# A four-layer cross-attention chain: wide attention scores for one head of two tiles per unit, the rarer expert as a weight difference, VectorE's softmax in half of all units

## The chip, the cores and the metric

The kernel runs on 1 core of one Trainium2 chip. The metric is the device time of that core in microseconds (us), from start to end of one execution. Engines are called PE (TensorE), DVE (VectorE), ACT (ScalarE), POOL (GpSimd) and SP (SyncE, which issues the transfers here).

## The reference

There are 64 batch entries of 64 tokens with 256 channels (x), and as many context tokens with 128 channels (ctx). Four layers follow each other.

```python
# L0: one-head attention of x over ctx @ W_mem, a sigmoid gate, RMS norm
# L1: LayerNorm, then 16 heads of 64 channels over ctx (masked), tanh-gated residual; LayerNorm, GELU MLP of 1024
# L2, L3, each:
vm  = expert_mask(types)                  # token and its successor are both of type 1
x   = rms_norm(h)
mixed = where(vm, x @ v_qkv, x @ l_qkv)   # 16 heads of 16 channels, rotary, causal attention
h   = h + where(vm, ctx @ v_dense, ctx @ l_dense)
h   = h + cross_attention(rms_norm(h))    # 16 heads of 8 channels over the context
mi  = rms_norm(h)
v_out = silu(mi @ v_gate) * (mi @ v_up) @ v_down
l_out = silu(mi @ l_gate) * (mi @ l_up) @ l_down     # 688 hidden channels
h   = h + where(vm, v_out, l_out)
```

In the inputs only tokens 48 to 63 of an entry can be of expert v; all others are of expert l. Everything is computed in f32.

## The kernel before

**Tiles and streams.** The 64 entries are eight groups of 8 entries (512 tokens; activations lie with channels on partitions, so a tile is 128x512). Two groups are in flight as streams a and b; four turns of both streams make the whole. Stream b runs about half a layer behind a, so that the attention of one stream lies beside the MLP of the other. In one turn the phases are, in this order: wide attention (L1) of a beside L0 of b; L1's MLP and L2 attention of a beside L1 of b; L2 attention of b beside the L2 MLP of a; L3 attention of a beside the L2 MLP of b; L3 attention of b beside the L3 MLP of a; L3 MLP of b beside L0 of the next a.

**Order.** `schedule` runs in Python when the program is made. It takes steps with nominal times (`l1_stage`, `attention_stage`, `ffn_stage` and so on), a cost table for each engine (`parts`) and dependencies (`follows`), and writes one fixed order of steps for each engine. Each engine then works its list strictly in that order and waits on semaphores. Where the planner expects PE to wait, it puts in filler products (`pause`, L966), whose results nobody reads.

**Wide attention, L1.** It has eight tiles j of two heads each (`l1_stage`). In each, `l1k` computes K (PE L1200, then two half-height ACT copies into a block-diagonal buffer, L1487, which `zero_k` on POOL has cleared, L1843), `l1v` computes V (L1211), `l1q` computes Q (L1220). `scores` makes one unit of 128x512: first the media mask as a bf16 product with 2 rows (L1013), then 8 products of 128 rows, 64 columns of weights and 128 streamed columns (L1017), which compute both heads at once thanks to the zeros in K. `prob` and `trans` (four transposes, L1057), `pv` (16 products in two 64x64 quarters, L1074) and `wo` (L1227) follow.

**Softmax.** There are two ways. ACT's way: DVE takes the maximum (L1639), ACT makes eight exponentials of 64 columns each with a sum (L1438). DVE's way (`by_vector`): DVE takes the maximum, subtracts it (L1644), ACT makes one exponential of 512 columns (L1431), DVE sums (L1653). Then DVE's reciprocal (L1655) and POOL's product (L1839) end both. Even units of L2 and L3 attention go DVE's way, and all of L1 goes ACT's. Four units fit into the buffer `Ebuf`. Units of L2 and L3 are made in pairs on two PSUM banks: the causal mask as two bf16 products of 64 rows (L1024), then 8 products of 64 rows, 64 weight columns and 256 streamed columns, which take the four 64x64 quarters in turn (L1033).

**Experts.** The activations are kept twice, masked: `xn` times `is_l` and `xv` times `is_v`. After a norm, DVE multiplies by the gains (`spread`, L1716), then by `is_l` (L1726 or L1729), then the late tokens by `is_v` (L1733), and POOL the others (L1853). PE adds l weights times `xn` and v weights times `xv`; for v only the 16 late tokens of each entry are streamed (L986, L1340, L1361). In the MLP, for each of 6 hidden chunks (`g`, `silu`, `u`, `down`): ACT copies g and takes a tanh, DVE makes the SiLU (L1796), multiplies by u (L1809), by `is_l` (L1814), the late tokens by `is_v` (L1815), and POOL the early tokens by `is_v` (L1881). `down` waits for these. MLP weights come from HBM through a ring of five slots (`load_chunk`, on SP), six transfers a chunk.

Of the kernel before, what the change touches and what calls it, by code (L numbers as in the profile page):

```python
# [14 lines left out]
P = 128  # L15
B, S, D, E = 64, 64, 256, 128
G = 8
# [47 lines left out]
def l0_stage():  # L65
    steps = [(0, "load"), (0, "masks"), (0, "x", 0), (0.5, "x", 1), (1.0, "ctx"), (3.0, "mem", 0), (3.9, "mem", 1),
             (4.8, "memN", 0), (5.7, "memN", 1), (7.0, "scores", ("l0", 0)), (9.5, "prob", ("l0", 0)),
             (12.0, "trans", ("l0", 0)), (14.0, "l0pv", 0), (15.0, "l0pv", 1), (16.0, "zero_k"), (17.0, "gate", 0),
# [4 lines left out]
def l1_stage():  # L73
    steps = []
    for j in range(JT):
        at = 8.7 * j
        steps += [(at, "l1k", j), (at + 0.9, "l1v", j), (at + 1.8, "l1q", j), (at + 3.9, "scores", ("l1", j)),
                  (at + 6.0, "prob", ("l1", j)), (at + 12.1, "trans", ("l1", j)), (at + 13.7, "pv", ("l1", j)),
                  (at + 24.5, "wo", j)]
# [3 lines left out]
    for j in range(JT):  # L83
        for k, (when, step) in enumerate(((0.5, ("trans", ("l1", j))), (2.0, ("pv", ("l1", j))), (5.0, ("wo", j)))):
            if step not in done:
                steps.append((end + when + 0.1 * j, *step))
# [50 lines left out]
def ffn_stage(n):  # L137
    steps = []
    for j in range(FT):
        steps += [(6.4 * j, "g", n, j), (6.4 * j + 1.5, "silu", n, j), (6.4 * j + 2.1, "u", n, j), (6.4 * j + 10.6, "down", n, j)]  # L140
    return steps + [(6.4 * FT + 6.4, "res3", n)], 6.4 * FT + 6.4
# [58 lines left out]
FILLER, HOP, SLACK, LEAD, REACH = 0.3, 0.2, 0.1, 10.0, 80.0  # L200
BULK = ("g", "silu", "u", "down", "l1h", "w2")
# [3 lines left out]
def parts(step, where):  # L205
# [6 lines left out]
    if step == "scores":  # L212
# [3 lines left out]
        if kind != "l1":  # L216
            return chain(("PE", 0.02 if where[0][2] % 2 else {"self": 1.35, "cross": 1.05}[kind]), *softmax)
        return chain(("PE", 1.35), *softmax)
# [12 lines left out]
    if step == "spread":  # L231
        own = chain(("PE", 0.3 if n in HALVED else 0.45), ("DVE", {0: 1.5, 1: 2.45, 2: 2.45, 4: 0.95, 7: 0.95, 5: 2.0, 8: 2.0}.get(n, 3.45)))
# [5 lines left out]
    if step == "keys":  # L238
        return [("POOL", 2.15, None)]
    if step == "u":  # L240
        return chain(*(() if where[1] == FT - 1 else (("PE", 2.2),)), ("DVE", 2.4), ("POOL", 1.4))
    if step == "g" and where[1] == FT - 1:
# [4 lines left out]
        "zero_k": (("POOL", 1.8),), "zero_s": (("POOL", 1.8),), "gate": (("PE", 3.45), ("ACT", 0.6)),  # L247
        "fuse": (("DVE", 1.4),), "mean": (("PE", 1.75), ("DVE", 1.4)), "l1k": (("PE", 0.9), ("ACT", 1.1)), "l1v": (("PE", 1.05), ("DVE", 0.65)),
# [1676 lines left out]
```

## Time and profile before

| what | value |
|---|---|
| median of 3 runs (lowest to highest) | 2722.21 us (2719.45 to 2730.94) |
| time of the profiled execution | 2724.13 us |
| its span in the trace | 2722.3 us |
| mean granted clock of PE | 0.994 of full speed |
| PE, DVE, ACT, POOL busy | 2627.3, 1624.8, 1318.6, 974.3 us |

The span counts from the first to the last instruction of the program; 1.8 us lie around it. A product in f32 stands as two records in the trace, each with its own weight load, so 8 products are "x16". Fillers count as busy PE time. In a timeline a row's duration includes the drain of the last product; the distance from one row's start to the next row's start is what the row costs.

### The profile page before, as it was taken

The numbers are of one execution on the slowest core, as the hardware profiler recorded it, in microseconds if no ns is written. First come the engines' busy times: TensorE is split into PE (matmuls) and PEld (weight loads), VectorE is DVE, ScalarE is ACT, GpSimd is POOL, SyncE is SP. The second block draws the span as 40 slices with busy tenths as digits, with TensorE's granted clock in tenths as the row PEclk, the third lists the DMA queues.
The fourth block names the chain that finished last, engine by engine and source line by source line (L and its number), as shares of the span: only waits on it lengthen the run. The fifth ranks groups of instructions, "written<-read, shape, count | busy, mean of one in ns | idle before, by whom it ended". The sixth has DMA issues, their size and how long they took to land.

```text
span 2722.3 us, 52680 instructions
## 1 busy us (share of the span) xinstructions
PE 2627.3 (97%) x19429; PEld 1584.6 (58%) x19429; DVE 1624.8 (60%) x3532; ACT 1318.6 (48%) x4818; POOL 974.3 (36%) x862
## 2 busy tenths in 40 slices
PE   6999999999999999999999999999999999999998
PEld 4556566665555656566556565656655556566664
DVE  2426567786424547777643454777855345477874
ACT  2446444654343644464444373555534447255452
POOL 0014344553111515555311241654621133155452
PEclk9999999999999999999999999999999999999999
DMA  7000021212201011120220101112121010120111
GB/s 204 1 24 13 21 55 36 52 29 71 67 1 36 2 31 51 30 64 22 70 63 1 35 2 47 43 30 55 29 71 55 1 36 2 51 58 19 48 29 55
DMA packets 171044, 109.52 MB, mean 40 GB/s; under 512 B 31714, under 2 KB 168356, under 8 KB 170660
## 3 DMA queue, kind: packets, MB, share of 16 engines
q1 hardware_dynamic: 166336, 105.82, 14.0%
q8 instruction: 160, 2.62, 0.4%
q10 hardware_dynamic: 4452, 0.29, 0.1%
q14 instruction: 96, 0.79, 0.1%
HBM read 101.87 MB, written 4.19 MB: 39 GB/s over the span
## 4 chain that ended last, share of the span: by engine, by line
PE 81%; DVE 10%; ACT 5%; issue 2%; POOL 1%; ACTq 1%; DVEq 0%
PE bank L1334 11%; PE bank L1351 6%; PE bank L979 5%; PE bank L1057 5%; PE bank L1239 4%; PE bank L1227 4%; PE bank L1248 4%; PE bank L1220 4%; PE bank L1274 3%; ACT Ebuf L1438 3%; PE bank L1340 3%; PE bank L1033 2%; PE bank L1074 2%; PE bank L1211 2%; PE bank L1017 2%
## 5 line engine op out<-in xcount | busy, mean ns | idle before, releaser
L1839 POOL TENSOR_TENSOR Ebuf<-Ebuf,row_rcp 128x512 f32<-128x512 f32 (+1 forms) x328 | 344.4, 1056 | 956.6 <-DVE row_rcp L1655 956.4
L1438 ACT ACTIVATE Ebuf<-bank,minus_max 128x64 f32<-128x64 f32 x1568 | 468.3, 333 | 116.3 <-DVE minus_max L1639 115.4
L1639 DVE TENSOR_REDUCE minus_max<-bank 128x8 f32<-128x512 f32 (+1 forms) x328 | 220.3, 674 | 226.2 <-PE bank L1017 124.5
L1438 ACT ACTIVATION_READ_ACCUMULATOR Ebuf<-bank,minus_max 128x1 f32 x1568 | 353.5, 225 | 0.0
L1447 ACT ACTIVATE PT<-bank 128x512 f32<-128x512 f32 (+1 forms) x328 | 193.7, 603 | 128.2 <-PE bank L1057 125.8
L1057 PE MATMUL bank<-ident,Ebuf 128*128 128x128 f32 x1296 | 200.9, 281 | 10.0 <-POOL Ebuf L1839 9.5
L1057 PEld LDWEIGHTS bank<-ident,Ebuf 128*128 128x128 f32 x1296 | 146.8, 142 | 79.2 <-issue 46.2
L1334 PE MATMUL bank<-xs_b,w_ring 128*128 128x512 f32 (+1 forms) x384 | 170.0, 605 | 2.4 <-DVE xs_b L1733 2.4
L1334 PE MATMUL bank<-xs_a,w_ring 128*128 128x512 f32 (+1 forms) x384 | 168.8, 602 | 0.0
L966 PE MATMUL bank<-causal_bf,ident_bf 128*128 128x512 bf16 x525 | 136.8, 383 | 0.0
L1881 POOL TENSOR_TENSOR arena_b<-arena_b,masks_b 128x384 f32<-128x384 f32 (+1 forms) x48 | 67.7, 1411 | 192.7 <-DVE arena_b L1809 192.6
L1431 ACT ACTIVATE Ebuf<-Ebuf 128x512 f32<-128x512 f32 x128 | 81.5, 637 | 91.0 <-DVE Ebuf L1644 89.3
L1655 DVE RECIPROCAL row_rcp<-row_sum 128x8 f32<-128x8 f32 (+1 forms) x328 | 65.1, 199 | 99.0 <-ACT Ebuf L1438 94.2
L1881 POOL TENSOR_TENSOR arena_a<-arena_a,masks_a 128x384 f32<-128x384 f32 (+1 forms) x48 | 61.2, 1278 | 139.6 <-DVE arena_a L1809 139.6
L1644 DVE TENSOR_TENSOR Ebuf<-bank,minus_max 128x512 f32<-128x512 f32 x128 | 88.6, 692 | 13.7 <-DVE minus_max L1639 0.5
L1653 DVE TENSOR_REDUCE row_sum<-Ebuf 128x8 f32<-128x512 f32 x128 | 86.5, 676 | 13.1 <-ACT Ebuf L1431 11.4
L1351 PE MATMUL bank<-arena_b,w_ring 128*128 128x512 f32 (+1 forms) x192 | 92.5, 603 | 1.8 <-DVE arena_b L1814 1.8
L1351 PE MATMUL bank<-arena_a,w_ring 128*128 128x512 f32 (+1 forms) x192 | 93.5, 609 | 0.0
L1334 PEld LDWEIGHTS bank<-xs_b,w_ring 128*128 128x128 f32 (+1 forms) x384 | 59.0, 180 | 58.0 <-issue 56.5
L1874 POOL TENSOR_TENSOR arena_b<-arena_b,head_rows 128x512 f32<-128x512 f32 x64 | 68.7, 1102 | 64.6 <-PE bank L1046 48.4
L1334 PEld LDWEIGHTS bank<-xs_a,w_ring 128*128 128x128 f32 (+1 forms) x384 | 58.6, 179 | 54.5 <-issue 53.5
L1184 PEld LDWEIGHTS bank<-ones,sq 128*128 128x128 f32 x576 | 73.9, 192 | 19.2 <-issue 12.2
(322 smaller groups left out, 5668.8 us busy)
## 6 DMA issues: line engine op xcount, KB each, us to landing
w_ring<-in_L_W SPq DMA_DIRECT2D x64, 256.0 KB, 3.1
w_ring<-in_L_l_gate SPq DMA_DIRECT2D x80, 128.0 KB, 2.2
w_ring<-in_L_l_up SPq DMA_DIRECT2D x80, 128.0 KB, 2.3
w_ring<-in_L_l_down SPq DMA_DIRECT2D x80, 128.0 KB, 2.2
w_ring<-in_L_v_gate SPq DMA_DIRECT2D x80, 128.0 KB, 2.4
w_ring<-in_L_v_up SPq DMA_DIRECT2D x80, 128.0 KB, 2.4
w_ring<-in_L_v_down SPq DMA_DIRECT2D x80, 128.0 KB, 2.5
arena_a<-in_x SPq DMA_DIRECT2D x4, 512.0 KB
```

What stands on the lines that cost most here:

```text
L966: mm(b[:, :].rearrange("p (h s) -> p h s", h=8), ident_bf[:, :], causal_bf[:, :].unsqueeze(1).broadcast_to([P, 8, S]), start=True, stop=True)
L979: mm(b, w_l[k], src_l[k], start=(k == 0), stop=(not every and k == DT - 1))
L1057: last = nc.tensor.transpose(b[:, c * P:(c + 1) * P], Ebuf[:, u % UNITS, c * P:(c + 1) * P], ident[:, :])
L1220: last = mm(b[:, :], w_q[:, k, j * P:(j + 1) * P], st.xn[:, k, :], start=(k == 0), stop=(k == DT - 1))
L1227: last = mm(acc[m][:, :], w_o[:, j, m * P:(m + 1) * P], st.l1_att[:, j % 2, :], start=(j == 0), stop=(j == JT - 1))
L1334: mm(to, of["l"][:, k, 0:rows], st.xn[:, k, :], start=(k == 0), stop=(not every and k == DT - 1))
L1351: mm(acc[m][:, :], w["l"][0:rows, m * P:(m + 1) * P], st.hid_l[0:rows, j % 2, :], start=(j == 0), stop=(not every and j == FT - 1), skip_g ...
L1438: last = A(Ebuf[:, u % UNITS, cell], bank(token)[:, cell], ACT.Exp, bias=minus_max[:, u % UNITS, c:c + 1], accum_out=row_sum[:, u % UNITS, ...
L1447: A(PT[:, t % 2, 0:width(key) * S], bank(token)[:, 0:width(key) * S], ACT.Copy).then_inc(pt_ready, 1)
L1639: V.reduce_max(minus_max[:, u % UNITS, 0:g], cells(bank(token)[:, 0:g * S]), AX_X, negate=True).then_inc(maxed, 1)
L1839: G_.tensor_tensor(v, v, row_rcp[:, n % 3, 0:g].unsqueeze(2).broadcast_to([P, g, S]), ALU.mult).then_inc(probs_ready, 1)
L1881: G_.tensor_tensor(by_batch(st.hid_v[0:rows, j % 2, :])[:, :, 0:LATE], by_batch(st.silu_g[0:rows, j % 2, :])[:, :, 0:LATE], by_batch(st.is ...
```

## The change

It has four parts.

- Wide attention: units come in pairs (`("l1", 1, i)`), and unit e of a pair holds head e of two tiles. K is stored as it is, four tiles deep, with one ACT copy; the block-diagonal buffer and `zero_k` are gone. For each pair two media-mask products of 64 rows go side by side, then 32 products of 64 rows, 64 weight columns and 64 streamed columns. `l1v` and the rows of `w_o` are laid out to match.
- Softmax: `by_vector` now holds for even units of L1 too.
- Experts: `xn`, and the hidden product, are no longer multiplied by `is_l`. Instead POOL subtracts the l weights from the v weights: in a new step `weigh` for each MLP chunk (three subtractions, before `g`), and once for the resident qkv and dense weights (in `zero_s` of stream a in turn 0).
- Late hidden tokens: POOL multiplies SiLU by `is_v` in the step `silu`, then DVE multiplies by u into `hid_v`. The planner learns of the new steps and of ring slots (`slot`).

```diff
 def l1_stage():
-        at = 8.7 * j
-        steps += [(at, "l1k", j), (at + 0.9, "l1v", j), (at + 1.8, "l1q", j), (at + 3.9, "scores", ("l1", j)),
+        at, e, key = 17.4 * (j // 2), j % 2, ("l1", 1, j)
+        steps += [(at + 2.6 * e, "l1k", j), (at + 2.6 * e + 0.9, "l1q", j), (at + 5.5 + 4.0 * e, "l1v", j),
+                  (at + 5.4 + 0.01 * e, "scores", key), ...
 def parts(step, where):
-        return chain(("PE", 1.35), *softmax)
+        return chain(("PE", 0.02 if where[0][2] % 2 else {"l1": 2.0, "self": 1.35, "cross": 1.05}[kind]), *softmax)
+    if step == "weigh":
+        return [("POOL", 1.7, None)]
-        return chain(*(() if where[1] == FT - 1 else (("PE", 2.2),)), ("DVE", 2.4), ("POOL", 1.4))
+        return chain(*(() if where[1] == FT - 1 else (("PE", 2.2),)), ("DVE", 1.0), ("POOL", 1.4))
-    return key[0] in PAIRED and key[2] % 2 == 0
-PAIRED = ("self", "cross")
+    return key[0] != "l0" and key[-1] % 2 == 0
+PAIRED = ("l1", "self", "cross")
 # scores, PE
-                    mm(sc[:, :]..., parity_bf[:, :], st.media_bias..., start=True, stop=True)
-                    for n in range(G):
-                        p, r = n // 2, n % 2
-                        last = mm(sc[64 * r:64 * r + 64, p * P:(p + 1) * P], st.l1_q[:, j % 2, n * S:(n + 1) * S],
-                                  st.l1_kbd[:, j % 2, n, :], start=False, stop=True, skip_group_check=True)
+                    for e, rows in enumerate(halves):
+                        mm(both[e]..., parity_bf[rows, :], st.media_bias[rows]..., start=True, stop=True)
+                    for p in range(PAIRS):
+                        for t in range(2):
+                            for r in range(2):
+                                n = 2 * p + r
+                                for e, rows in enumerate(halves):
+                                    last = mm(both[e][64 * r:64 * r + 64, p * P + t * S:p * P + (t + 1) * S], st.l1_q[rows, (i + t) % 4, n * S:(n + 1) * S],
+                                              st.l1_k[rows, (i + t) % 4, n * S:(n + 1) * S], start=False, stop=True, skip_group_check=True)
 # qk and g, PE
-                            pe.wait_ge(w_loaded[n], 16 * 9)
+                            pe.wait_ge(w_weighed, n - 1)
-                            pe.wait_ge(*there)
+                            pe.wait_ge(*weighed[s].at(turn, FT * (n - 2) + j + 1))
 # l1k, ACT
-                    for r in range(2):
-                        last = A(st.l1_kbd[64 * r:64 * r + 64, j % 2, :, 64 * r:64 * r + 64], by_batch(b[64 * r:64 * r + 64, :]), ACT.Copy)
+                    A(st.l1_k[:, j % 4, :], bank(token)[:, :], ACT.Copy).then_inc(l1_k_ready[s].sem, 1)
 # spread, DVE
-                    if n in (3, 6):
-                        for m in range(DT):
-                            V.tensor_tensor(st.xn[:, m, :], st.xv[:, m, :], st.is_l[:, :], ALU.mult)...
-                    if n in (5, 8):
-                        V.tensor_tensor(st.xn[:, :, at], st.xv[:, :, at], both(st.is_l[:, at]), ALU.mult)...
 # u, DVE
-                    V.scalar_tensor_tensor(out=v, in0=v, scalar=0.5, in1=up, ...).then_inc(h_ready[s].sem, 1)
-                    V.tensor_tensor(st.hid_l[0:rows, j % 2, :], v, st.is_l[0:rows, :], ALU.mult).then_inc(hl_ready[s].sem, 1)
-                    V.tensor_tensor(by_batch(st.hid_v...)[:, :, LATE:S], by_batch(v)[:, :, LATE:S], by_batch(st.is_v...)[:, :, LATE:S], ALU.mult)...
+                        dve.wait_ge(*hv_early[s].at(turn, k - 1))
+                    V.scalar_tensor_tensor(out=st.hid_l[0:rows, j % 2, :], in0=v, scalar=0.5, in1=up, ...).then_inc(h_ready[s].sem, 1)
+                    dve.wait_ge(*sv_ready[s].at(turn, k + 1))
+                    V.scalar_tensor_tensor(out=hv, in0=hv, scalar=0.5, in1=by_batch(up)[:, :, LATE:S], ...).then_inc(hv_late[s].sem, 1)
 # POOL
+                    if turn == 0 and s == 0:
+                        for n in (2, 3):
+                            for of in (w_qkv, w_dense):
+                                last = G_.tensor_tensor(rare, rare, other, ALU.subtract)
+                if step == "weigh":
+                    pool.wait_ge(*there)
+                    for of in "gu":
+                        G_.tensor_tensor(rare, rare, other, ALU.subtract)
+                    G_.tensor_tensor(down["v"]..., down["v"]..., down["l"]..., ALU.subtract).then_inc(weighed[s].sem, 1)
+                if step == "silu":
+                    pool.wait_ge(*silu_ready[s].at(turn, k + 1))
+                    G_.tensor_tensor(by_batch(st.hid_v...)[:, :, LATE:S], by_batch(st.silu_g...)[:, :, LATE:S],
+                                     by_batch(st.is_v...)[:, :, LATE:S], ALU.mult).then_inc(sv_ready[s].sem, 1)
```

## Rows read from the trace of the kernel before

**Rows 1.** The page's first part: span, busy time of the engines.
```profile
span 2722.3 us, 52680 instructions
PE 2627.3 (97%) x19429; PEld 1584.6 (58%) x19429; DVE 1624.8 (60%) x3532; ACT 1318.6 (48%) x4818; POOL 974.3 (36%) x862
```

**Rows 2.** Windows, five phases of turn 2: length, busy (instructions) per engine, clock, DMA.
```profile
1402.00:1528.00 126.00, 124.98 (x884) 70.95 (x884) 42.06 (x96) 54.92 (x195) 12.50 (x11) 1.00 0.09 28
1528.00:1692.00 164.00, 160.12 (x1279) 94.09 (x1278) 83.41 (x195) 89.63 (x359) 54.92 (x51) 0.99 0.08 22
1692.00:1805.00 113.00, 108.42 (x806) 66.93 (x805) 85.91 (x180) 57.55 (x207) 57.02 (x49) 1.00 0.17 46
1805.00:1900.00 95.00, 92.47 (x747) 59.24 (x746) 74.58 (x166) 53.19 (x202) 51.65 (x45) 1.00 0.17 46
1900.00:2005.00 105.00, 101.47 (x781) 63.43 (x779) 82.95 (x173) 54.47 (x204) 54.86 (x48) 1.00 0.19 49
```

**Rows 3.** Groups of PE by form, the fillers: count, busy us, mean ns, idle.
```profile
L966 PE MATMUL bank<-causal_bf,ident_bf 128*128 128x512 bf16 x525 | 136.8, 383 | 0.0
```

**Rows 4.** Timeline of PE, two L1 units and an L2 pair: start, duration.
```profile
1559.86 0.39 PE L1013 MATMUL bank<-media_b,parity_bf 2*128 2x512 bf16 x1
1560.18 1.09 PE L1017 MATMUL bank<-arena_b 128*64 128x128 f32 x16
1561.20 1.13 PE L1274 MATMUL bank<-w_l_qkv,xs_a 128*128 128x256 f32 x4
...
1567.85 0.39 PE L1024 MATMUL bank<-causal_bf,ident_bf 64*128 64x512 bf16 x2
1568.17 1.09 PE L1033 MATMUL bank<-arena_a 64*64 64x256 f32 x16
...
1575.24 1.15 PE L1074 MATMUL bank<-PT,arena_b 64*64 64x64 f32 x32
1576.32 0.45 PE L1083 MATMUL bank<-PT,arena_a 128*32 128x64 f32 x16
1576.70 0.38 PE L1013 MATMUL bank<-media_b,parity_bf 2*128 2x512 bf16 x1
```

**Rows 5.** Groups of DVE by form: busy us, mean ns, idle before.
```profile
L1639 DVE TENSOR_REDUCE minus_max<-bank 128x8 f32<-128x512 f32 x320 | 216.9, 681 | 221.8 <-PE bank L1017 124.5 <-PE bank L1046 50.2 <-PE bank L1033 46.5
L1644 DVE TENSOR_TENSOR Ebuf<-bank,minus_max 128x512 f32<-128x512 f32 x128 | 88.6, 692 | 13.7 <-DVE minus_max L1639 0.5
...
L1815 DVE TENSOR_TENSOR arena_a<-arena_a,masks_a 128x128 f32<-128x128 f32 x40 | 41.9, 1049 | 0.0
...
L1814 DVE TENSOR_TENSOR arena_a<-arena_a,masks_a 128x512 f32<-128x512 f32 x40 | 34.4, 859 | 1.4
...
L1729 DVE TENSOR_TENSOR xs_b<-xs_b,masks_b 128x512 f32<-128x512 f32 x16 | 12.6, 785 | 0.6
...
L1733 DVE TENSOR_TENSOR xs_a<-xs_a,masks_a 128x128 f32<-128x128 f32 x16 | 4.7, 292 | 0.5
```

**Rows 6.** Timeline of DVE at the start of an L3 attention.
```profile
1899.86 1.41 DVE L1716 SCALAR_TENSOR_TENSOR xs_b<-xT_b,gains,bank 128x512 f32<-128x512 f32 x2 [0.22 <-PE bank L1193]
1901.18 1.29 DVE L1726 TENSOR_TENSOR xs_b<-xs_b,masks_b 128x512 f32<-128x512 f32 x2
```

**Rows 7.** Groups of ACT by form: an exponential, a half copy of K.
```profile
L1438 ACT ACTIVATE Ebuf<-bank,minus_max 128x64 f32<-128x64 f32 x1568 | 468.3, 333 | 116.3 <-DVE minus_max L1639 115.4
...
L1487 ACT ACTIVATE arena_b<-bank 64x512 f32<-64x512 f32 x64 | 38.2, 596 | 16.7 <-PE bank L1200 16.3
```

**Rows 8.** Groups of POOL by form.
```profile
L1839 POOL TENSOR_TENSOR Ebuf<-Ebuf,row_rcp 128x512 f32<-128x512 f32 x320 | 339.5, 1067 | 880.7 <-DVE row_rcp L1655 880.4
...
L1853 POOL TENSOR_TENSOR xs_a<-xs_a,masks_a 128x192 f32<-128x192 f32 x32 | 23.2, 743 | 58.1 <-DVE xs_a L1729 58.1
...
L1839 POOL TENSOR_TENSOR Ebuf<-Ebuf,row_rcp 128x256 f32<-128x256 f32 x8 | 4.9, 612 | 75.9 <-DVE row_rcp L1655 75.9
```

More of the change, by code:

```diff
@@ L252, in parts @@
         "ckeys": (("POOL", 2.15),), "dense": (("PE", 2.5), ("DVE", 0.65)), "cq": (("PE", 0.9), ("ACT", 0.4)), "cdense": (("PE", 1.0), ("DVE", 0.65)),
-        "g": (("PE", 2.2), ("ACT", 1.1)), "silu": (("DVE", 0.9),), "down": (("PE", 2.2),), "out": (("PE", 0.5), ("ACT", 0.55)),
+        "g": (("PE", 2.2), ("ACT", 1.1)), "silu": (("DVE", 0.9), ("POOL", 0.45)), "down": (("PE", 2.2),), "out": (("PE", 0.5), ("ACT", 0.55)),
         "store": (("SP", 3.0),), "load": (("SP", 5.0),)}[step])
@@ L367, in schedule @@
     norm = None
+    chunks = []
     holds, bank_of, held_by = [None] * (BANKS - 2) + [("table", 0, 0)] * 2, {}, {}
@@ L403, in room @@
         key = where[0] if where else None
+        if step == "weigh":
+            return slot()
+        if step == "l1h" and where[0] % 2 == 0:
+            there, free = slot(), banks(1)
+            return None if there is None or free is None else max(there, free)
         if step in FILL_STEPS and parts(step, where)[0][0] == "PE":
@@ L486, in schedule @@
             heads[step, s].pop()
+            if step == "weigh":
+                chunks.append((("ffn", s, turn, *where), ("down", s, turn, *where)))
+            if step == "l1h" and where[0] % 2 == 0:
+                chunks.append((("f1", s, turn, where[0] // 2), ("w2", s, turn, where[0] + 1)))
             for j, (other, _, follow) in enumerate(pieces):
@@ L933, in _ @@
             resident(1, w_q[:, :, :], tiles(a["L1_Wq"]))
-            resident(1, w_o[:, :, :], tiles(a["L1_Wo"]))
+            for t in range(2):
+                for e in range(2):
+                    rows = a["L1_Wo"].rearrange("(j t e d) n -> t e d j n", t=2, e=2, d=L1_HD)[t, e]
+                    resident(1, w_o[64 * t:64 * t + 64, e:JT:2, :], rows)
             for token in ORDER["SP"][:SLOTS]:
@@ L1319, in stages @@
                         rows = P if j < FT - 1 else FR
-                        ring, there = chunk("ffn", s, turn, n, j)
+                        ring, _ = chunk("ffn", s, turn, n, j)
                         w = ffn_weights(ring)[0][step]
@@ L1874, in _ @@
                         G_.tensor_tensor(*cross_blocks(st, p, r), ALU.mult).then_inc(kbd_built[s].sem, 1)
+                if step == "weigh":
+                    n, j = where
+                    rows = P if j < FT - 1 else FR
+                    ring, there = chunk("ffn", s, turn, n, j)
+                    into, down = ffn_weights(ring)
+                    pool.wait_ge(*there)
+                    for of in "gu":
+                        rare, other = (into[of][e][:, :, 0:rows] for e in "vl")
+                        G_.tensor_tensor(rare, rare, other, ALU.subtract)
+                    G_.tensor_tensor(down["v"][0:rows, :], down["v"][0:rows, :], down["l"][0:rows, :], ALU.subtract).then_inc(weighed[s].sem, 1)
+                if step == "silu":
+                    n, j = where
+                    rows, k = P if j < FT - 1 else FR, FT * (n - 2) + j
+                    pool.wait_ge(*silu_ready[s].at(turn, k + 1))
+                    if j >= 2:
+                        pool.wait_ge(*down_done[s].at(turn, k - 1))
+                    G_.tensor_tensor(by_batch(st.hid_v[0:rows, j % 2, :])[:, :, LATE:S], by_batch(st.silu_g[0:rows, j % 2, :])[:, :, LATE:S],
+                                     by_batch(st.is_v[0:rows, :])[:, :, LATE:S], ALU.mult).then_inc(sv_ready[s].sem, 1)
                 if step == "u":
```

221 lines of the change are left out of this document (112 added, 109 removed).

## Prediction

> **What bounds the kernel now.** I read the page's first part, then windows by phase, then PE's groups. PE is busy for 2627.3 of 2722.3 us [rows 1] and at full clock in every phase [rows 2]. Of that busy time, 136.8 us are fillers, 525 products that nobody reads [rows 3], put where the planner expected PE to wait. So waiting is 95.0 us of idle time plus 136.8 of filler, 232 us or 8.5%, and 2490 us are products that are needed. The reader should see two things. First, whatever takes needed products away from PE is gained at its full price: in the first phase (L1 of one stream beside L0 of the other) PE idles for 1.0 us in 126, and DVE, ACT and POOL are busy for 42, 55 and 13 us [rows 2]. Second, in the three phases in which one stream's attention lies beside the other's MLP, DVE is 76 to 79% busy and PE idles for 4.6, 2.5 and 3.5 us [rows 2]. This makes 10.6 us a turn and 42 in all. With fillers shared out by length (these phases are 46% of the span, an estimate) another 63 us are there, 105 us of waiting in sum. DVE's relief can work only on this part.
>
> **The change part by part.** The sum is made against the profiled execution, 2724.1 us (span 2722.3), 1.9 us above the median of the three runs.
>
> *Wide scores on PE.* Start to start, a unit costs 0.32 us for the media mask (1559.86 to 1560.18) and 1.02 for its 16 records (to 1561.20) [rows 4]. Two units, which is what a new pair replaces, cost 2.68 us. The new pair has two mask products of 64 rows on two banks, the form of the causal mask: 0.32 us for both (1567.85 to 1568.17) [rows 4]. Then come 32 products, so 64 records of 64 streamed columns in the four 64x64 quarters in turn. No row shows this form. L1033 streams as many columns in all (16 x 256 = 64 x 64) in the same order of quarters, in the 1.09 us that L1017's row prints too, so in 1.02 from start to start [rows 4]: this is the low end. L1083 has 64-column records in four column quarters, 16 in 0.38 us (1576.32 to 1576.70), 24 ns each with the start of the block in it [rows 4]; 64 of these would take 1.5 us. L1074, with two quarters, has 32 records in 1.08 us (1575.24 to 1576.32), so 2.16 for 64 [rows 4]: the high end, no better than the two blocks that go. I take 1.1 us, near L1033, which it is nearest to in quarters and order. A pair then costs 1.42 and saves 1.26 us; there are 32 pairs (8 groups, 4 each): **-40 us**, ends -42 and -6. The planner of the change itself counts 2.0 us for a pair; that would be -22. All of it lies on PE, which is the bound there.
>
> *The norm in front of qkv.* PE's first l product waited for L1716 twice and then L1726. The pair of gains takes 1.41 us from 1899.86, and L1726's pair 1.29 from 1901.18 [rows 6]. Now it waits for the first gain alone: one L1716 and one L1726 earlier, 1.3 us. There are 16 such starts. Another stream's work covers about half of them, which I judge by the phase ends: **-11 us**, ends 0 and -21. *The norm in front of the MLP* loses one L1729, 0.79 us [rows 5], 16 times, half covered: **-6**, ends 0 and -13.
>
> *DVE in the MLP.* L1814 (0.86) and L1815 (1.05) go, and a late product of 128x128 comes, for which L1733 shows 0.29 [rows 5]: 1.6 us less a chunk. Of six chunks a phase that is 10 of about 83 us, so DVE falls from 77% to 68%. What that gives back is the least certain term. Attention's chain in the other stream stands in DVE's queue for a shorter time, but POOL, ACT and PE steps in it stay. I take somewhat over a quarter of the 105 us: **-30**, ends 0 and -60.
>
> *ACT and softmax.* K's copy is one instead of two of 0.60 us [rows 7]. Half of L1's units need one exponential in place of eight of 0.33 [rows 7], while DVE gets L1644's 0.69 [rows 5] and a sum of about the same length as L1639's 0.68. That is 32 x 1.4 = 44 us more on DVE, at 33 and 51% in the two L1 phases [rows 2]. I cost both at nothing: PE's work hides them. If that cover were gone, a pair's chain would be longer by 1.4 us and shorter by ACT's exponentials, so hardly different. The new layout of `l1v`, the one attention buffer moved into `xv`, `w_o` in four transfers instead of one and SP's same ring transfers cost nothing; the first phase's loads come long before `w_o` is used.
>
> *POOL.* `weigh` is three subtractions of up to 256 columns, for which L1839's 128x256 form shows 0.61 us [rows 8]: 1.8 us a chunk. The late SiLU product has 128 columns; L1853's 192 take 0.74 [rows 8], so about 0.5. Over 96 chunks that is 220 us; POOL goes from 974 [rows 1] to about 1190 us, and from 52% to 65% in the three phases. Everything queued behind these on POOL (L1839's probabilities, the keys, the rotary product) may start later. Of DVE's two-source operations that read SBUF, some 25 a phase, an eighth more would meet POOL, each for about 0.6 us, and a quarter of that is on the path: 25 x 16 phases x 0.13 x 0.6 x 1/4 = **+8**, ends 0 and +30. That such meetings cost shows in one form at two prices: 128x128 takes 1.05 us beside POOL's L1881 and 0.29 alone [rows 5]. The Trainium skill ("SBUF — State Buffer", Who interferes with whom) says that a DVE instruction with two SBUF inputs is shut out for the whole of a GpSimd instruction that reads SBUF. By that rule the new late product, whose second input is in PSUM, goes free while the rotary sums pay more; it would raise my +8 but not turn it round.
>
> *New waits.* PE's g waits for POOL's weights, and DVE, inside u, for POOL's late SiLU, with all of DVE's list behind it. The planner puts weigh up to 9 us ahead and silu 0.6 us before u, so most are covered by u's own products on PE; I take **+6**, ends 0 and +80 (the slower rival). The resident weights (4096 columns, 8 x 1.07 = 8.5 us [rows 8]) block POOL once, with stream b's first probabilities behind: **+3**, ends 0 and +8.
>
> Sum: -40 - 11 - 6 - 30 + 8 + 6 + 3 = -70. 2724 - 70 = **2654 us**, or 2652 if set against the median.
>
> **The rivals.**
> - *The row halves do not go side by side.* Then quarters with the same columns load their weights one after the other, and 64 records run at L1074's pace: that part gives -6 instead of -40, and the time is 2688. For it speaks that no row has four 64x64 quarters with short streams; against it that L1033 gets four quarters' worth in the time of two [rows 4]. The Trainium skill ("TensorE: Matmul & The Clock Gate", Step-by-step: what each phase is for) says that row tiling uses no further operand bus, while column tiling does, and gives a weight load as columns/1.2 ns. On that estimate loads go in twos, 32 x 53 ns = 1.7 us a pair, and this part would give -21 us.
> - *The relief is worth more.* If DVE was what kept attention behind in the three phases, over half of the 105 us goes, and the norms' full price with it: 2724 - 40 - 21 - 13 - 60 + 17 = 2607.
> - *Pairs are coarser.* Two L1 units are now made at once in a buffer of four, beside attention's pairs. If each of 32 pairs makes PE wait for 1 us for a transpose, and POOL's queue eats the relief, what is left is 2724 - 40 - 17 + 32 + 7 = 2706, about no change. For it: the second phase idles for 3.9 us already [rows 2]. Against: the softmax engines have half of that phase free.
> - *Slower: POOL comes too late in `u`.* DVE stands still inside u until POOL has done the late SiLU. If a chunk's product finds one L1839 (1.07 us [rows 8]) or a weigh in front of it, and DVE's stop reaches PE, each of 96 chunks pays about 1.2 us: +115 in place of the +6, so 2654 + 109 = 2763. It decides against the change from (70 + 6)/96 = 0.8 us a chunk. For it: strictly fixed lists and POOL at 65%. Against: POOL idles for 35% in each phase, and u's own PE products take 2 us in which POOL can act.
>
> **How the numbers follow.** Forecast 0.48 (2630 to 2678), row halves in sequence 0.16, more relief 0.10, coarse pairs 0.14, POOL late 0.12. A measurement can tell from no change about 0.5%, 14 us, so no change is 2709 to 2736. Faster is all of the first three but 0.01, and just over half of coarse pairs: 0.82. No change takes the rest of coarse pairs and a mild form of late POOL: 0.09. Slower takes the rest: 0.09. The range goes from 2605, which holds more relief, to 2712, which leaves out late POOL and the upper part of coarse pairs.
>
> **What would show it.** In the changed profile: the L1 score block of 64 records at 1.0 to 1.2 us from start to start (2.1 would be the first rival), 32 blocks; needed PE work down by 40 us; no DVE operation of 1.05 us in u and DVE near 1480 us; POOL near 1190; ACT down by about 90. Right steps would leave waiting (idle and fillers) near 190 us. A DVE wait inside u on POOL that is longer than 0.8 us in most chunks, or PE waits on `weigh`, would make the forecast wrong.

## The result and the profile after

The changed kernel takes **2686.8 us** (median of 4 runs, 2684.61 to 2689.42); the kernel before, beside it, 2720.83. The ratio is 0.9875, 95% interval 0.986 to 0.989. That is faster by 34 us: the right sign and inside the range of 2605 to 2712, but half of the 70 us that I forecast, and outside the 2630 to 2678 that I had given to the forecast without its rivals. The profiled execution took 2684.68 us.

The page's first part, kernel after. It answers to [rows 1].

```profile
span 2682.8 us, 54240 instructions
PE 2560.8 (95%) x20342; PEld 1554.7 (58%) x20342; DVE 1534.7 (57%) x3448; ACT 1222.7 (46%) x4274; POOL 1155.9 (43%) x1242
```

PE groups by form, kernel after: fillers, then the new wide scores and their masks.

```profile
L982 PE MATMUL bank<-causal_bf,ident_bf 128*128 128x512 bf16 x414 | 109.3, 384 | 0.0
...
L1039 PE MATMUL bank<-arena_b 64*64 64x64 f32 x1024 | 18.6, 221 | 0.0
L1039 PE MATMUL bank<-arena_a 64*64 64x64 f32 x1024 | 18.6, 221 | 0.0
```

Idle time is 2682.8 - 2560.8 = 122.0 us, fillers are 109.3: **231.3 us of waiting, where before had 231.8** [rows 1, 3]. The work that is needed fell from 2490.5 to 2451.5. So PE has less to do by 39 us, and not one microsecond of waiting went; I had expected it to fall to 190.

The timeline of PE shows the new pair. Masks at 1554.83, scores at 1555.15, the next work at 1556.24: 0.32 + 1.09 = 1.41 us, where two units took 2.68 [rows 4].

```profile
1554.83 0.39 PE L1031 MATMUL bank<-media_b,parity_bf 64*128 64x512 bf16 x2
1555.15 1.16 PE L1039 MATMUL bank<-arena_b 64*64 64x64 f32 x64
1556.24 0.66 PE L1081 MATMUL bank<-ident,Ebuf 128*128 128x128 f32 x4
```

Windows of turn 2, kernel after, cut at like events as in [rows 2]: length, busy (instructions) of PE, PE's loads, DVE, ACT, POOL, then clock and DMA.

```profile
1391.00:1500.00 109.00, 108.76 (x942) 63.22 (x942) 42.87 (x97) 39.01 (x114) 10.60 (x10) 1.00 0.08 24
1500.00:1658.00 158.00, 151.98 (x1400) 90.38 (x1399) 89.65 (x199) 78.83 (x291) 57.55 (x54) 0.99 0.08 23
1658.00:1771.00 113.00, 108.89 (x806) 68.10 (x805) 74.00 (x171) 57.57 (x208) 69.52 (x73) 0.98 0.17 46
1771.00:1873.00 102.00, 97.98 (x765) 63.14 (x764) 73.36 (x170) 54.25 (x203) 65.18 (x74) 0.98 0.16 43
1873.00:1974.00 101.00, 95.23 (x745) 59.90 (x744) 69.17 (x147) 51.98 (x200) 63.33 (x67) 0.98 0.14 38
```

The two phases with wide attention got shorter, but only the second can be compared: the planner moved the border of the first, which now holds three of the four new pairs where it held all eight units. The last three, in which DVE was to be relieved, took 313 us before [rows 2] and take 316 now, though DVE is down from 76 to 79% to 65 to 72%. Together they hold the same needed products in both kernels, and 54 fillers (15.0 us) where there were 74 (19.1 us). PE's idle time in them went up from 10.6 to 13.9 us, and the clock went down from 1.00 to 0.98 of full speed. So waiting, idle time and fillers together, is 28.9 us where it was 29.7. DVE's relief did next to nothing for it. The needed products took 287.1 us instead of 283.3, at the lower clock.

PE's waits, kernel after: line, what it waited for, us in total, times, longest.

```profile
PE bank L1217 <- DVE norm_a L1731: 25.3, 18, 2.0
PE bank L1217 <- DVE norm_b L1731: 20.4, 20, 2.6
PE bank L1358 <- POOL w_ring L1909: 11.2, 8, 1.8
PE bank L1081 <- POOL Ebuf L1861: 9.4, 9, 2.1
```

In the kernel before the same view says:

```profile
PE bank L1193 <- DVE norm_b L1702: 13.2, 26, 1.0
PE bank L1057 <- POOL Ebuf L1839: 9.5, 20, 1.3
...
PE bank L1193 <- DVE norm_a L1702: 2.4, 5, 1.3
```

The first product of a norm's `spread` (L1217, before L1193) waits for the last of nine small DVE operations that make 1/sqrt of the variance (L1711 to L1731, before L1682 to L1702): 45.7 us instead of 15.6. The 11.2 us in front of the gate product are new. Groups of DVE by form, kernel after:

```profile
L1717 DVE TENSOR_TENSOR norm_a<-norm_a 128x2 f32<-128x2 f32 x32 | 18.7, 583 | 1.1
L1714 DVE TENSOR_SCALAR norm_a<-norm_a 128x2 int32<-128x2 int32 x32 | 14.4, 450 | 1.1
...
L1719 DVE TENSOR_TENSOR norm_a<-norm_a 128x2 f32<-128x2 f32 x32 | 12.8, 399 | 1.1
...
L1837 DVE SCALAR_TENSOR_TENSOR arena_a<-arena_a,bank 128x128 f32<-128x128 f32 x40 | 11.2, 279 | 0.0
...
L1726 DVE TENSOR_TENSOR norm_a<-norm_a 128x2 f32<-128x2 f32 x32 | 5.2, 161 | 1.1
```

An operation on two columns takes 160 ns alone and 583 in the mean at L1717 of stream a. All 936 of these operations sum to 233.3 us, before to 180.1; 154 of them last over 300 ns, before 44. At L1717 and L1719, which have both operands in SBUF, the 68 operations that overlap a two-input instruction of POOL all last over 300 ns, and the other 140 at most 165. Why, the timeline of DVE and POOL together shows, kernel after, in one norm of stream b (start, duration):

```profile
1919.90 4.04 POOL L1899 TENSOR_TENSOR arena_b<-arena_b,head_rows 128x512 f32<-128x512 f32 x4 [2.14 <-ACT arena_b L1547]
...
1920.52 0.16 DVE L1711 TENSOR_SCALAR norm_b<-bank 128x2 f32<-128x2 f32 x1
1920.71 0.25 DVE L1714 TENSOR_SCALAR norm_b<-norm_b 128x2 int32<-128x2 int32 x1
...
1921.00 0.96 DVE L1717 TENSOR_TENSOR norm_b<-norm_b 128x2 f32<-128x2 f32 x1
...
1921.99 0.96 DVE L1719 TENSOR_TENSOR norm_b<-norm_b 128x2 f32<-128x2 f32 x1
...
1922.99 0.97 DVE L1721 SCALAR_TENSOR_TENSOR norm_b<-norm_b 128x2 f32<-128x2 f32 x1
...
1923.89 1.41 POOL L1908 TENSOR_TENSOR w_ring<-w_ring 128x256 f32<-128x256 f32 x2
1923.99 0.65 DVE L1724 TENSOR_TENSOR norm_b<-norm_b 128x2 f32<-128x2 f32 x1
...
1924.67 0.65 DVE L1726 TENSOR_TENSOR norm_b<-norm_b 128x2 f32<-128x2 f32 x1
1925.26 0.73 POOL L1909 TENSOR_TENSOR w_ring<-w_ring 128x256 f32<-128x256 f32 x1
1925.36 0.65 DVE L1728 SCALAR_TENSOR_TENSOR norm_b<-norm_b 128x2 f32<-128x2 f32 x1
```

POOL makes four instructions of 1.0 us without a break, then the three subtractions of a chunk. DVE's chain gets through **one step for each POOL instruction**: starts at 1921.00, 1921.99, 1922.99, then 0.7 us apart while POOL subtracts. The chain takes 5.7 us where it would take 1.8, and PE's next `spread` product came after 2.63 us of idling. The subtractions stand directly behind POOL's other work and so prolong the stretch in which it has no gap.

### The profile page after: what moved, and what is told of

Read it like the earlier page. It is cut to its first block, busy times and chain, and to the rows that moved or that the text cites. A ratio compares the mean times of both kernels' runs of the same rounds, so it can differ in the third digit from the quotient of the medians.

```text
span 2682.8 us, 54240 instructions
## 1 busy us (share of the span) xinstructions
PE 2560.8 (95%) x20342; PEld 1554.7 (58%) x20342; DVE 1534.7 (57%) x3448; ACT 1222.7 (46%) x4274; POOL 1155.9 (43%) x1242
## 4 chain that ended last, share of the span: by engine, by line
PE 82%; DVE 11%; POOL 2%; issue 2%; ACT 1%; ACTq 1%; DMA 0%; SPq 0%; DVEq 0%
PE bank L1358 10%; PE bank L1375 6%; PE bank L1081 6%; PE bank L995 5%; PE bank L1244 4%; PE bank L1251 4%; PE bank L1263 4%; PE bank L1272 4%; PE bank L1364 3%; PE bank L1116 2%; PE bank L1298 2%; PE bank L1098 2%; PE bank L1057 2%; PE bank L1224 2%; PE bank L1070 2%
## 5 line engine op out<-in xcount | busy, mean ns | idle before, releaser
L1463 ACT ACTIVATE Ebuf<-bank,minus_max 128x64 f32<-128x64 f32 x1312 | 392.4, 334 | 39.8 <-DVE minus_max L1668 39.5
L1463 ACT ACTIVATION_READ_ACCUMULATOR Ebuf<-bank,minus_max 128x1 f32 x1312 | 297.4, 227 | 0.0
L1456 ACT ACTIVATE Ebuf<-Ebuf 128x512 f32<-128x512 f32 x160 | 102.0, 638 | 101.6 <-DVE Ebuf L1673 99.5
L1908 POOL TENSOR_TENSOR w_ring<-w_ring 128x256 f32<-128x256 f32 x192 | 131.9, 708 | 0.0
L1673 DVE TENSOR_TENSOR Ebuf<-bank,minus_max 128x512 f32<-128x512 f32 x160 | 110.7, 692 | 16.9 <-DVE minus_max L1668 0.5
L1682 DVE TENSOR_REDUCE row_sum<-Ebuf 128x8 f32<-128x512 f32 x160 | 107.9, 675 | 8.6 <-ACT Ebuf L1456 7.8
L982 PE MATMUL bank<-causal_bf,ident_bf 128*128 128x512 bf16 x414 | 109.3, 384 | 0.0
L1878 POOL TENSOR_TENSOR xs_a<-xs_a,masks_a 128x192 f32<-128x192 f32 (+1 forms) x48 | 36.2, 774 | 133.4 <-DVE xs_a L1745 133.4
L1817 DVE SCALAR_TENSOR_TENSOR arena_b<-arena_b 128x512 f32<-128x512 f32 (+1 forms) x48 | 42.7, 889 | 76.2 <-ACT arena_b L1581 76.0
L1899 POOL TENSOR_TENSOR arena_b<-arena_b,head_rows 128x512 f32<-128x512 f32 x64 | 65.5, 1056 | 42.5 <-PE bank L1070 28.9
```

The lines of the kernel that those rows point to most:

```text
L982: mm(b[:, :].rearrange("p (h s) -> p h s", h=8), ident_bf[:, :], causal_bf[:, :].unsqueeze(1).broadcast_to([P, 8, S]), start=True, stop=True)
L1463: last = A(Ebuf[:, u % UNITS, cell], bank(token)[:, cell], ACT.Exp, bias=minus_max[:, u % UNITS, c:c + 1], accum_out=row_sum[:, u % UNITS, ...
L1673: V.tensor_tensor(cells(Ebuf[:, u % UNITS, 0:g * S]), cells(bank(token)[:, 0:g * S]), minus_max[:, u % UNITS, 0:g].unsqueeze(2).broadcast_ ...
L1682: V.reduce_sum(row_sum[:, u % UNITS, 0:g], cells(Ebuf[:, u % UNITS, 0:g * S]), AX_X).then_inc(summed, 1)
L1908: G_.tensor_tensor(rare, rare, other, ALU.subtract)
```

## Experiments

**Theory A**: `weigh` and what it shifts on POOL hold up the norm's small operations, which are on PE's path; this eats the relief of DVE. **Rival B**: the expert part costs by work that comes late on POOL (the subtraction before `g`, SiLU in `u`), whatever the norm does. **Rival C**: the parts in L1 cost something, and the expert part is free. (Each recorded expectation names theories of its own; its letters hold for it alone.)

One caution for all differences below. The planner writes a new order of steps wherever steps or their costs change. The order and the fillers are the same in the change, weigh_tiny, weigh_writes, chain_psum and chain_weigh_tiny, and also in before and before_chain_psum, and in scores_only and scores_chain; in scores_vector and scores_vector_chain they are the same but for five places. A difference inside such a group is the edit's own. A difference between groups has a new order in it. What that is worth was not measured by itself; chain_plan and plan_costs, at the end, each moved the time by 7 us with a new order alone.

**scores_only**, the wide scores alone: the expert hunks taken back, and

```diff
-    return key[0] != "l0" and key[-1] % 2 == 0
+    return key[0] not in ("l0", "l1") and key[-1] % 2 == 0
```

> The wide scores alone: pairs, one K copy, no block-diagonal buffer, but L1's softmax all ACT's way and the experts as before. Theory A (the whole gain is PE's shorter score block, 32 pairs x 1.26 us, and the expert part is worth nothing): about 2681 us, 40 below the kernel before, and no slower than the full change. Rival B (pairs of units in a buffer of four make PE wait, and the expert part hides that): 2700 us or more, with more PE waiting for transposes of L1.

2675.64 us, ratio 0.9838 (0.9818 to 0.9859), so -45 against 2720.97. PE's L1 score products and masks fell from 85.8 to 44.9 us (summed start to start, without PE's idle time behind three of the blocks). This part alone gives more than the whole change. It came out 5 us below the recorded 2681; PE's waiting hardly moved (103.4 us idle and 126.4 us of fillers, 229.8 against 231.8), so no cost of pairs in a buffer of four shows.

**experts_only**: the expert hunks alone (`xn` and the hidden product no longer times `is_l`, `weigh`, the late SiLU on POOL), wide attention as before.

> The experts' weight difference alone, with its new POOL steps; scores and L1 softmax as before. Theory A (DVE's relief is given back by POOL: the norms' small DVE operations and the MLP's first weights are held up): 2715 to 2735 us, no change, with the small norm operations of DVE at 220 us or more in sum against 180 before. Rival B (the relief works by itself and only the pairs spoil it): 2700 us or less.

2746.18 us, ratio 1.0082 (1.0054 to 1.0109): **slower** than before by 25. Its runs differ by their granted clock: five at 0.986 to 0.989 took 2744.7 to 2751.2, two at 0.997 and 0.996 took 2728.7 and 2732.7. The kernel before took 2714.2 to 2719.4 in its runs at 0.997, so at a like clock 9 to 15 of the 25 us stay, and the rest goes with the clock; it gained in no run. That is worse than the 2715 to 2735 that I expected of theory A, and its norm operations sum to 213.6 us and not 220 or more. Rival C falls. Its waits of PE show the same two causes as the full change:

```profile
PE bank L1206 <- DVE norm_b L1714: 21.6, 21, 2.6
...
PE bank L1206 <- DVE norm_a L1714: 11.5, 13, 2.1
PE bank L1347 <- POOL w_ring L1896: 11.1, 8, 1.8
```

**weigh_tiny**: the full change, the three subtractions of a chunk left out (late v tokens come out other).

```diff
-                    for of in "gu":
-                        rare, other = (into[of][e][:, :, 0:rows] for e in "vl")
-                        G_.tensor_tensor(rare, rare, other, ALU.subtract)
-                    G_.tensor_tensor(down["v"][0:rows, :], down["v"][0:rows, :], down["l"][0:rows, :], ALU.subtract).then_inc(weighed[s].sem, 1)
+                    G_.memset(down["v"][0:rows, 0:1], 0.0).then_inc(weighed[s].sem, 1)
```

> The full change, but POOL's three subtractions of an MLP chunk are replaced by clearing one column of the down weights, so the MLP's v weights stay undiminished (the output for late v tokens is another one). Same order of steps on every engine. Theory A (POOL's 2.3 us a chunk cost both in front of g and through DVE's norms): 2660 us or less, PE's wait for POOL's weights at 0, norm operations of DVE at 200 us or less in sum against 233. Rival C (they lie beside other work, the lost relief is the planner's order): within 8 us of the full change, 2679 to 2687.

2648.1 us, ratio 0.9735 (0.9715 to 0.9756). The subtractions cost 38.7 us; PE's waits for the norm fall from 45.7 to 26.6, the norm's operations sum to 201.0 us, and the wait for `w_ring` is gone. A and B both allow this much.

```profile
PE bank L1217 <- DVE norm_a L1731: 18.1, 13, 2.0
...
PE bank L1217 <- DVE norm_b L1731: 8.5, 14, 1.2
```

**chain_psum**: the full change, with the norm's small operations written so that none has two operands in SBUF. The bank that the sums came in holds w, step_a and step_b; y*y*w becomes (y*w)*y; there is one operation more. The planner is told that the bank is held for 1.8 us and not 0.25; order and fillers stay, and only the choice of PSUM banks changes, which was not tested by itself.

```diff
-                    w, y, step_a, step_b = (v[:, some] for v in (st.minus_half_var, st.rstd, st.step_a, st.step_b))
+                    w, step_a, step_b = (bank(token)[:, 64 * c:64 * c + count] for c in range(1, 4))
+                    y, again = st.rstd[:, some], st.step_b[:, some]
...
-                    V.tensor_tensor(step_a, y, y, ALU.mult).then_inc(step_done.sem, 1)
+                    V.tensor_tensor(step_a, y, w, ALU.mult).then_inc(step_done.sem, 1)
...
-                    V.tensor_tensor(step_b, step_a, w, ALU.mult).then_inc(step_done.sem, 1)
+                    V.tensor_tensor(step_b, step_a, y, ALU.mult).then_inc(step_done.sem, 1)
```

> The full change, but the small operations of the norm keep w and the products in the PSUM bank of the sums, so that none of them reads two operands from SBUF (one operation more a norm, and the bank is held until the chain ends). Theory A (POOL's reads of SBUF hold up DVE operations with two SBUF inputs, and that is what PE's spread waits for): norm operations of DVE at 190 us or less in sum against 233, PE's idle wait for the norm at 20 us or less against 46, 2665 us or less. Rival C (the norms come late for other reasons): sum falls little and the time stays within 5 us of 2687.

**2634.61 us**, ratio 0.969 (0.967 to 0.971): 52 us faster than the change, with the same work on POOL. In the profiled executions PE's idle time falls from 122.0 to 80.6 us, which is nearly all in its waits for the norm, and its busy time from 2560.8 to 2550.9. The timeline of DVE and POOL at the same place as above:

```profile
1884.58 4.03 POOL L1902 TENSOR_TENSOR arena_b<-arena_b,head_rows 128x512 f32<-128x512 f32 x4 [2.14 <-ACT arena_b L1547]
...
1885.20 0.17 DVE L1713 TENSOR_SCALAR bank<-bank 128x2 f32<-128x2 f32 x1
1885.40 0.16 DVE L1716 TENSOR_SCALAR norm_b<-bank 128x2 int32<-128x2 int32 x1
...
1885.60 0.17 DVE L1719 TENSOR_TENSOR bank<-norm_b,bank 128x2 f32<-128x2 f32 x1
...
1886.85 0.16 DVE L1734 SCALAR_TENSOR_TENSOR norm_b<-bank,norm_b 128x2 f32<-128x2 f32 x1
```

Beside the same four POOL instructions the chain now takes 1.8 us. Its 1040 operations sum to 169.8 us, none over 300 ns, and of PE's waits for the norm 7.1 us are left:

```profile
PE bank L1358 <- POOL w_ring L1912: 9.6, 9, 1.8
...
PE bank L1217 <- DVE norm_b L1734: 4.3, 9, 0.6
PE bank L1217 <- DVE norm_a L1734: 2.8, 4, 0.7
```

**weigh_writes**: the subtractions replaced by 12 clears of the v weights, so POOL writes as much and reads nothing (the v part adds nothing).

```diff
-                        G_.tensor_tensor(rare, rare, other, ALU.subtract)
+                        for k in range(DT):
+                            for c in range(2):
+                                G_.memset(into[of]["v"][:, k, c * rows // 2:(c + 1) * rows // 2], 0.0)
```

> The full change, but POOL's three subtractions of an MLP chunk are replaced by twelve small clears of the v weights, about 1.8 us of POOL time a chunk that only writes (the experts' v part then adds nothing for the chunk, so the output is another one). Same order of steps. Theory A as it now stands (reading by POOL holds up DVE's two-input operations, which is most of the 39 us that weigh costs; its time on POOL costs the rest): norm operations of DVE near 205 us in sum as without the subtractions (201) and not 233, and a time of 2650 to 2665 us. Rival C (POOL's time in front of g and of its other steps is what costs): 2675 to 2690 us, whatever the norm operations do.

2656.06 us, ratio 0.9782 (0.9764 to 0.9799), 8 more than weigh_tiny. POOL is busy for 1058 us, halfway from weigh_tiny's 966 to the change's 1156, so the clears are shorter than the subtractions, and the time alone proves little. What the norm's lines did is sharper. The two-operand lines L1717 to L1728 are as in weigh_tiny, within 1 us each (L1717 34.5 against 33.8 us); only L1714, one operand in and out of SBUF, went up, from 35.4 to 45.5. One by one: 58 operations of L1719 to L1731 overlap clears and nothing else of POOL, and none lasts over 165 ns. Nine of L1714 do, and they last 762 to 810 ns, through up to ten clears that start 0.09 us apart. Groups of DVE by form, weigh_writes:

```profile
L1714 DVE TENSOR_SCALAR norm_a<-norm_a 128x2 int32<-128x2 int32 x32 | 20.9, 652 | 1.1
L1717 DVE TENSOR_TENSOR norm_a<-norm_a 128x2 f32<-128x2 f32 x32 | 14.4, 450 | 1.1
```

and weigh_tiny:

```profile
L1717 DVE TENSOR_TENSOR norm_a<-norm_a 128x2 f32<-128x2 f32 x32 | 14.4, 450 | 1.1
L1714 DVE TENSOR_SCALAR norm_a<-norm_a 128x2 int32<-128x2 int32 x32 | 13.5, 423 | 1.1
```

So two-operand operations are held up by POOL's two-input instructions, which read SBUF, and not by its clears, which only write. The single-source one is held up by clears as well.

**before_chain_psum**: the same edit of the norm on the kernel before.

> The kernel before with the norm's small operations in the PSUM bank of the sums and nothing else changed. Theory A (the hold-up of DVE by POOL's reads was there before the change too, and grew with it): norm operations at 160 us or less in sum against 180, time 2690 to 2708 us, so a smaller gain than the 52 us that it brings on top of the change. Rival D (PSUM access alone makes these operations quicker, by the same on any kernel): the same 50 us, 2670 us.

2711.2 us, ratio 0.9971 (0.9961 to 0.9981). Only 8 to 10 us, less than the 12 to 30 of my expectation: before, POOL seldom met the chain (44 operations over 300 ns). The sum of the norm's operations fell from 180.1 to 169.4 us and not below 160. So PSUM by itself does not give 50 us on any kernel.

**scores_vector**: scores_only and the vector half in all units (`by_vector` as in the change).

> The wide scores with half of L1's units DVE's way, experts as before. Theory A (DVE and ACT both have room in the L1 phases): within 4 us of the wide scores alone (2676), 2672 to 2680. Rival E (the 44 us more on DVE are what spoils the full change): 2685 us or more.

2664.78 us, ratio 0.9813 (0.9795 to 0.983): the vector half gives 11 us, outside the 2672 to 2680 that I had expected. The expert part on top makes 2686.8, so it costs 22.

**scores_chain**: scores_only with the norm in PSUM.

> The wide scores alone plus the norm's small operations in PSUM; experts and softmax as before. Theory A (the expert part gives something once POOL's reads no longer reach the norms): slower than the full change with the same norm (2635), 2640 to 2660 us. Rival F (the expert part costs in any case, since POOL's weights are waited for in front of g): 2630 us or less, the best version so far.

2654.86 us, ratio 0.9769 (0.9751 to 0.9787), 21 us faster than scores_only: the norm's place is worth 8 to 10 us on the kernel before, 21 with the wide scores, 52 with the expert part as well.

**scores_vector_chain**: all but the expert part, the norm in PSUM.

> The wide scores and the vector half in all units, with the norm's small operations in PSUM, and the rarer expert in the first form (no subtraction of weights). It stands against chain_psum (2634.6), which has the subtractions as well. Theory A (the expert part lost its 22 us because POOL's reads of SBUF held up the norm's small operations; with those in PSUM that loss is gone): this kernel is no faster than chain_psum, 2638 to 2652 (scores_chain's 2654.9 less the vector half's 11 gives 2644). Rival B (the expert part costs by POOL's work in front of the first gate product and by the POOL queue, whatever the norm does): this kernel is faster than chain_psum by 10 or more, below 2625. Between 2628 and 2638: the expert part is then worth nothing either way.

2642.81 us, ratio 0.9727 (0.9708 to 0.9747). Now the expert part is worth 2642.81 - 2634.61 = 8 us of **gain**, where with the norm in SBUF it cost 22. Both differences hold the same new order, so the 30 us between them are the norm's; the 8 us are no more than what a new order can move. The sign turns with the place of w, step_a and step_b; rival B said below 2625.

**chain_weigh_tiny**: chain_psum without the subtractions (edit and outputs as in weigh_tiny).

> chain_psum with the three subtractions of each chunk left out, one small clear in their place (the outputs of the late v tokens come out other). It shows what the subtractions still cost when the norm's small operations are in PSUM; with the norm in SBUF leaving them out gave 38.7 us (2686.8 to 2648.1). Theory A: most of the 38.7 was the norm's chain; what is left is the wait of the first gate products for the subtraction (9.6 us in chain_psum's waits) and a little of other VectorE operations, so 2615 to 2626. Rival B (the price of the subtractions is their lateness on POOL, not the norm): again 30 us or more, 2605 or below. If the norm's chain was all of it and the gate wait is hidden: 2628 to 2635.

2622.08 us, ratio 0.9639 (0.9622 to 0.9655). The subtractions cost 12.5 us here against 38.7 there. So 26 of the 38.7 went through the norm. The rest is the work coming late, which the 9.6 us wait for `w_ring` nearly covers. B has a third of the cost, A two thirds.

**chain_plan** and **plan_costs**: chain_psum, and the change, with the planner's costs set to what the traces show.

```diff
-        return chain(("PE", 0.02 if where[0][2] % 2 else {"l1": 2.0, "self": 1.35, "cross": 1.05}[kind]), *softmax)
+        return chain(("PE", 0.02 if where[0][2] % 2 else {"l1": 1.4, "self": 1.35, "cross": 1.05}[kind]), *softmax)
...
-        return [("POOL", 1.7, None)]
+        return [("POOL", 2.35, None)]
```

(plan_costs also has 2.5 for 1.8 on DVE in `sums`.)

> chain_psum with two costs of the planner set to what the traces show: wide scores 1.4 us a pair on PE (the plan has 2.0), the subtraction of a chunk 2.35 us on POOL (the plan has 1.7). If the order around the scores is what leaves PE waiting (late v products, transposes), 2620 to 2630. If the order is near enough already, 2630 to 2640. An order that comes out worse by chance: up to 2655.

> The changed kernel with three costs of the planner set to its own trace: wide scores 1.4 us, the norm's small operations 2.5 us (the plan has 1.8, both normed streams took about 2.2 and more), the subtraction 2.35 us. Theory A's second half (PE waits for the norm because the plan places the product that spreads the norm too early, so other work could fill the longer chain): the waits of PE for the norm fall from 45.7 us and the time to 2662 to 2678. Rival: the operations are on the path whatever the order, because nothing else is ready then: 2680 to 2692.

2642.04 us, ratio 0.9714 (0.9698 to 0.973), 7 worse than chain_psum, in the part that I had left to an order that is worse by chance; and 2693.89 us, ratio 0.991 (0.9893 to 0.9926), 7 worse than the change and just above the 2680 to 2692 of the rival: the 2662 to 2678 that I had expected missed. In plan_costs PE's waits for the norm did fall, from 45.7 to 24.7 us. But the planner filled the longer chain with products that nobody reads:

```profile
L982 PE MATMUL bank<-causal_bf,ident_bf 128*128 128x512 bf16 x566 | 150.6, 389 | 0.0
```

Fillers went from 109.3 to 150.6 us: the planner put nothing else in the place of the wait, and the wait became filler. Idle time and fillers together rose from 231.3 to 253.8 us.

## Why the prediction came out as it did

In numbers, each difference from the runs above (the first three rows are between kernels with different orders, so some us in each are not the term's own; the fourth is not):

| term | forecast | measured |
|---|---|---|
| wide scores | -40 | -45 |
| ACT and softmax | 0 | -11 |
| norms shorter and DVE relief, chunk subtractions absent | -11 - 6 - 30 | -17 (2664.8 to 2648.1) |
| subtractions, meetings on POOL, new waits | +8 + 6 + 3 | +39 (2648.1 to 2686.8) |
| sum | -70 | -34 |

(The third row holds the late SiLU and the resident weights too, since weigh_tiny keeps them.)

- **Wide scores**: right, and by its own steps: a pair took 1.41 us where I took 1.42, in 32 pairs, and 40.9 us came off PE's work. The other 4 us of the 45 are not assigned. The choice of L1033 as the nearest row held, since the four quarters with short streams do go side by side. The load figure of the Trainium skill ("TensorE: Matmul & The Clock Gate", LDWEIGHTS (loading the stationary operand)), which I had taken two at a time for 1.7 us, would have given -21 for this part. 64 records in 1.09 us are 17 ns each, so by an estimate from that figure, 53 ns a load, about three loads must overlap. The statement of the Trainium skill ("TensorE: Matmul & The Clock Gate", Step-by-step: what each phase is for) that row tiling needs no further bus is in line with it; my step from it to "in twos" was not.
- **ACT and softmax at nothing**: wrong by 11. The exponentials were not hidden throughout. DVE's reciprocal waited 110.5 us for them in scores_only and 52.1 in scores_vector. On PE the gain is 7 us of fillers (from 488 to 462 of them), which the planner saved since its plan has a shorter softmax, and 4 us of idle time (103.4 to 99.3).
- **The relief**: sized wrong. DVE did what I said: L1814 and L1815 of the kernel before are gone, and L1837 takes 279 ns and never waits. DVE's busy time, 1534.7 us, is my 1480 and the 53 us by which the norm's operations grew, within 2 us. But "somewhat over a quarter of 105 us" took a busy share for a cause of waiting. With the norm in PSUM and no subtractions, which is the best case for this part, it gives 2642.8 - 2622.1 = 21 us, norms included, where I had 47. That even this much is due to DVE is not shown, for the order is another one too.
- **POOL's meetings**: this is the step that failed. I counted about 25 two-source operations a phase, took an eighth more of them as meeting POOL, and **a quarter of that as on the path**: +8, ends 0 and +30. The operations that matter are nine dependent ones in a row. A meeting there is no single delay of 0.6 us: while POOL works without a break, every step waits for the end of the POOL instruction that runs. And a large part of it is on the path, since `spread` on PE waits for the last: the norm's operations grew by 53.2 us over the kernel before, and PE's waits for them by 30.1. The price of the subtractions through the norm alone is 26 us, and the term as a whole, forecast at +17 with the new waits and the resident weights, measured +39. The Trainium skill ("SBUF — State Buffer", Who interferes with whom) had the rule, and the traces agree in each form: L1717 of stream a (two operands in SBUF) 583 ns in the mean where 160 is its time alone, L1673 (one of two in PSUM) 692 ns beside POOL as well as alone, clears by POOL without effect on two-operand lines. I cited it for the rotary sums and did not ask which chain on PE's path is made of such operations.
- **New waits**: PE's wait for `weigh` is there (11.2 us, 8 times), since a chunk's subtractions take 2 x 0.763 + 0.773 = 2.3 us and not my 1.8. The slower rival's mechanism did not come: L1837 idles for 0.0 us.
- **Other rivals**: coarse pairs would show in PE's wait for `Ebuf`, which is 9.4 us as before (9.5).

That the total still came within the range owes something to chance: softmax gave 11 us that were not in the sum, against the 52 us by which the relief and POOL's terms missed together (30 and 22). And 2686.8 is nearer to the 2688 of the first rival, row halves in sequence, than to my 2654; its mechanism did not come, as the 1.41 us of a pair show.

The clock enters too. In the three phases it is 0.98 after and 1.00 before; in chain_psum's (111, 100 and 96 us long) it is 1.00, 0.98, 1.00. I ran nothing that changes the clock alone, but the profiled executions bound it. Of chain_psum's 51 us, 41.4 are idle time of PE, of which its waits for the norm are 38.6; only the 9.9 us by which PE's busy time fell can hold the clock itself, and the mean granted clocks of 0.993 and 0.995 make some 5 us of it, an estimate (0.002 of 2683). Whether the lower clock comes from the added waits is left open.

## What to carry to other kernels

Before work is moved to GpSimd, find the chains of small dependent VectorE operations in front of the bound engine, and look where their operands lie: with two in SBUF, each step can take as long as one GpSimd instruction. Putting one operand in a PSUM bank, held a little longer for it, costs at most some 10 ns a step and gave here 52 us, more than the change itself; on the kernel before, where POOL seldom met the chain, the same edit gave 8 to 10. And an engine's busy share is no measure of what relief is worth: ask which wait ends last on it.

## What the runs showed of the hardware

- A 128x2 VectorE operation with both operands in SBUF takes 160 ns, up to 1.18 us beside GpSimd instructions that read SBUF; with one operand in PSUM 148 to 171 ns (all 1040 of the norm in chain_psum, of two or four columns), beside the same GpSimd work.
- A single-source `tensor_scalar` on SBUF, even of two columns, is held up too, and by instructions of GpSimd that only write (L1714: 35.4 to 45.5 us in sum; 170 ns alone, 762 to 810 beside clears), while 58 two-operand steps beside such clears last at most 165 ns.
- GpSimd itself was not slowed by this in the stretch shown: its four instructions took 4.04 us beside the SBUF form and 4.03 beside the PSUM form.
- 64 records (32 f32 products) of 64x64 weights and 64 streamed columns, in the four quarters in turn, take 1.09 us; 32 such records in two quarters take 1.08 us [rows 4].
